# Attention kernel on one NeuronCore: the row maxima enter the shifted scores through the product itself instead of through a second product

## The chip, the cores and the metric

The program runs on 1 core of one Trainium2 chip. The metric is the device time of one execution in microseconds (us), lower is better.

## The reference

Two transformer-like layers over 4096 tokens of width 128, all in fp32. The change lies in the attention of layer 1: 32 sequences of 128 tokens, 16 heads of 8 channels.

```python
x = x + moe0(modulated(x))                      # layer 0: experts, top 2 of 8
x = x + adapter(x)                              # layer 1
h = layernorm(x, ln1_g, ln1_b)
q, k, v = split(h @ w_qkv + b_qkv, 3)           # per head: [128 tokens, 8]
scores = einsum('bhqd,bkhd->bhqk', q, k) / sqrt(8)
attn = softmax(scores, axis=-1)
x = x + einsum('bhqk,bkhd->bqhd', attn, v).reshape(B, S, D) @ w_o + b_o
x = x + moe1(layernorm(x, ln2_g, ln2_b))        # router, top 2 of 8, experts
```

The kernel computes exp(score minus the maximum of its row), so a maximum per query and head must reach the scores before the exponential.

## The kernel before

The program is a row of stages: setup, the router and experts of layer 0, `pre_attention` (adapter, layer norm, queries and keys, written to DRAM), `attention` with the layer norm, router and scatter behind it (`Post`), `experts1`, `finish`. Within a stage each engine runs its own instruction list in the order in which the code writes it; semaphores (`wait_ge`, `then_inc`) join the lists. There is no scheduler.

Inside `attention` the work goes in **laps**, `for s in range(LAPS)`, one lap for each of 32 sequences and 14 more to drain. The 16 heads of a sequence are four groups `g` of four heads. A query or key side of a group is 96 partitions (a high part, a low part and the high part again, 32 rows each, so that one fp32r product is exact enough). What lap s does:

- TensorE (PE), for g = 0 to 3: `score(s + 2, g)`, a 96-row product of queries with masked keys `km` into `ps1`, for the maxima; `shift(s, g)`, the keys `kp` times the masked queries `qm` into `ps2` (line 1721) and then, into the same bank, `selr` times `mxT` (line 1723), which subtracts the maxima. Behind g = 0 stands `mix(s - 1)`, behind g = 3 `total(s - 1)`, 16 small products each. Behind g = 1 stands `turn_max(s + 1)`, four transposes that bring the maxima of the next sequence into `psM`; behind g = 2 `project(s - 2)`.
- VectorE (DVE): `maximum(s + 2, g)` (line 1577, TENSOR_REDUCE of a bank of `ps1` into `mneg`), `invert`, `divide`, `keep` of sequence s - 2.
- ScalarE (ACT): `exponent(s, g)` (line 1662), `copy_max(s + 1)` (line 1648, `psM` to `mxT`, 128x512) between the exponents of g = 1 and 2, and `mask_k(s + 3, j)` for j = 1, 2, 3 (line 1655, `kp` to `km`), the first ahead of the exponent of g = 1, the others behind the copy and behind the exponent of g = 2.
- GpSimd (POOL): `part_max(s + 1)` (lines 1525 and 1527, the maxima split in a high and a low part), `mask_k(s + 3)` for j = 0 (line 1515), `spread_v(s)`, then what the router needs: `post_root`, two indirect scatters (line 472), `post_join`.
- SyncE (SP): in pairs of sequences, 12 loads of `qm` (line 1505) once `shifted` says that the pair two back is done, and then the 6 loads of `qp` and `kp` of the next pair (line 1010).

`score(s, 0)` waits in `ready(s)` for all of `km` of its sequence: for ACT's j = 3 of the lap before it among others. The router work of four sequences is spread over laps by `group(s, after)`. From lap 7 on the laps repeat in four kinds, which the prediction names by letters:

- **T** (s = 7, 11, ...): ACT normalises behind the exponent of g = 2, and PE ends the lap with `post_turn`.
- **S** (s = 8, 12, ...): ACT scales, and PE ends the lap with `post_natural` (line 1403), which uses the banks `psW` and `psM` and waits for `kept` of this lap and for the maxima to have left `psM`.
- **R** (s = 9, 13, ...): DVE takes the logits, ACT copies two row halves (line 461) ahead of its first `mask_k`, DVE picks experts.
- **P** (s = 10, 14, ...): PE ranks, DVE takes statistics and places; its `index_sum` (line 453) gives the indices for which POOL's scatters wait, and `project` waits for DVE's line 436.

Laps 0 to 6 have little or none of that; they are called plain.

```python
for g in range(HG):            # PE, the order within a lap
    if s + 2 < SEQS:
        score(s + 2, g)
    if s < SEQS:
        shift(s, g)
    if behind and g == 0:
        mix(s - 1, range(4))
    if behind and g == 3:
        total(s - 1, range(4))
```

Of the kernel before, what the change touches and what calls it, by code (L numbers as in the profile page):

```python
# [16 lines left out]
P = 128  # L17
SEQS = 32
# [999 lines left out]
def pre_attention(m, d):  # L1018
# [3 lines left out]
    with ExitStack() as ctx:  # L1022
# [29 lines left out]
        with nc.Block(no_gpsimd_drain=True) as block:  # L1052
# [66 lines left out]
            def _(dve):  # L1119
# [23 lines left out]

                dve.wait_ge(m.late_ld, LATE_LOADS)
# [297 lines left out]
def attention_loads(m, ctx):  # L1442

    m.qp, m.kp = ([m.sb(f"{x}{b}", [96, HG, PAIR], F32R, ctx) for b in range(PAIR_BUFFERS)]
                  for x in ("qp", "kp"))
    m.pair_in = m.sems(*(f"a_pair{b}" for b in range(PAIR_BUFFERS)))


def attention(m, d):
# [3 lines left out]
    with ExitStack() as ctx:  # L1453
        sb = lambda n, s, dt=F32: m.sb(n, s, dt, ctx)
        two = lambda n, s, dt=F32: [m.sb(f"{n}{b}", s, dt, ctx) for b in range(2)]
        selr = sb("selr", [P, HG, P], F32R)
        qp, kp, pair_in = m.qp, m.kp, m.pair_in
        qm = two("qm", [96, HG, 4, PAIR], F32R)
# [4 lines left out]
        mxT = two("mxT", [P, 4 * P], F32R)  # L1463
# [6 lines left out]
        (cleared, made, km_pool, km_act, vb_done, scored, maxed, link, parted, turned, mxT_done, shifted,  # L1470
         exped, mixed, divided, projected, kept) = m.sems(
            "a_cleared", "a_made", "a_km_pool", "a_km_act", "a_vb", "a_scored", "a_maxed", "a_link", "a_parted",
            "a_turned", "a_mxT", "a_shifted", "a_exped", "a_mixed", "a_divided", "a_projected", "a_kept")
        qm_in = m.sems("a_qm_in0", "a_qm_in1")
        zeroed = m.sems("a_zeroed0", "a_zeroed1")
# [4 lines left out]
        side = lambda s: (s // 2) % PAIR_BUFFERS  # L1480
        PAIRS = SEQS // 2
# [7 lines left out]
        with nc.Block(no_gpsimd_drain=True) as block:  # L1489
            @block.sync  # L1490
            def _(sp):
                for k in range(PAIRS):
# [16 lines left out]
            def _(pool):  # L1509
                def mask_k(s):  # L1510
# [3 lines left out]
                    for j in range(KM_POOL):  # L1514
                        ins = nc.gpsimd.tensor_scalar(km[s % 2][:, :, j, :], kp[side(s)][:, :, tok(s)].bitcast(F32),  # L1515
# [24 lines left out]
                nc.gpsimd.memset(qm[1][:].bitcast(F32), 0.0).then_inc(zeroed[1], 1)  # L1540
# [29 lines left out]
            def _(dve):  # L1570
# [8 lines left out]

                def invert(s):  # L1580
# [12 lines left out]
                nc.vector.memset(qm[0][:].bitcast(F32), 0.0).then_inc(zeroed[0], 1)  # L1593
                for g in range(HG):
                    ins = nc.vector.tensor_copy(selr[:, g, :], bc(m.const[:, C_SEL + g:C_SEL + g + 1], P, P))
                ins.then_inc(cleared, 1)
                for s in range(2):
                    for g in range(HG):
                        maximum(s, g)
                for s in range(LAPS):  # L1600
# [397 lines left out]
```

## Time and profile before

| what | value |
|---|---|
| median of 3 runs | 771.48 us (765.51 to 772.9) |
| profiled execution, its own time | 765.54 us |
| its span, first to last instruction | 763.7 us |
| attention stage, first score product to the last exponent | about 331 to 557 us of the span |
| busy over the span | PE 79%, DVE 63%, POOL 59%, ACT 50% |
| mean granted TensorE clock | 0.912 of full speed |

Times on the rows of the next section are microseconds from the start of the span, means are ns. PE rows are modelled at their ends, so the distance from the start of one matmul to the start of the next says what it holds of the engine, and its duration says more than that. On a row "[0.20 <-ACT km L1655]" means that the engine had sat idle for 0.20 us and what ended the wait.

### The profile page before, as it was taken

How to read it: one execution, taken by the hardware profiler on the slowest of the kernel's cores; microseconds unless marked ns; L12 is line 12 of the kernel's file. 1: busy time of each engine (PE TensorE's matmuls, PEld its weight loads, DVE VectorE, ACT ScalarE, POOL GpSimd, SP SyncE). 2: the span in 40 equal slices, each digit the busy share in tenths (PEclk: the TensorE clock that was granted, in tenths of full speed). 3: DMA queues.
4: the chain of work that ended last, by engine and by line, in shares of the span. 5: the costliest groups of instructions: out<-in, count | busy, mean ns of one | idle time of the engine just before them, and what ended most of it. 6: DMA issues, size and time to landing. Idle time of an engine off the chain costs nothing. (4 is left out here: it accounts for less than half of the span.)

```text
span 763.7 us, 18100 instructions
## 1 busy us (share of the span) xinstructions
PE 600.0 (79%) x5634; PEld 483.7 (63%) x5634; DVE 480.4 (63%) x1470; ACT 384.6 (50%) x828; POOL 449.0 (59%) x588
## 2 busy tenths in 40 slices
PE   2999935999991767559899989999960699999950
PEld 1566625988991544327666666666740699999950
DVE  2555544766672699655557657656734487878835
ACT  1543403655560334246777777778640365555620
POOL 2477761766677556193545777777666056666650
PEclk9999976999995799959999999999975699999985
DMA  5921155777763168635454563564414988888519
GB/s 162 273 60 49 49 105 153 209 195 205 210 188 113 50 204 220 236 60 88 80 110 71 102 130 81 109 120 93 89 40 99 298 271 242 255 245 253 156 49 317
DMA packets 97833, 115.24 MB, mean 151 GB/s; under 512 B 16128, under 2 KB 77600, under 8 KB 97632
## 3 DMA queue, kind: packets, MB, share of 16 engines
q1 hardware_dynamic: 82224, 92.36, 46.9%
q0 software_dynamic: 9088, 18.76, 7.7%
q10 hardware_dynamic: 6448, 3.20, 1.8%
q8 instruction: 38, 0.62, 0.4%
q14 instruction: 35, 0.29, 0.1%
HBM read 80.75 MB, written 33.53 MB: 150 GB/s over the span
## 5 line engine op out<-in xcount | busy, mean ns | idle before, releaser
L472 POOL DMA_INDIRECT dispatch_rows<-row,index x128 | 128.1, 1000 | 62.4 <-issue 33.9
L1577 DVE TENSOR_REDUCE mneg<-ps 128x4 f32<-128x512 f32 x128 | 87.6, 687 | 77.1 <-PE ps L1711 76.9
L833 POOL DMA_INDIRECT expert_rows<-fo,to x78 | 84.0, 1077 | 68.4 <-DVE fo L1884 55.0
L833 POOL DMA_INDIRECT expert_rows<-eo,to x78 | 74.8, 959 | 50.0 <-ACT eo L926 28.1
L1662 ACT ACTIVATE prob<-ps 128x512 f32<-128x512 f32 x128 | 75.7, 592 | 40.8 <-PE ps L1723 40.3
L806 DVE CAST xh<-psT 128x256 fp32r<-128x256 f32 x78 | 33.1, 425 | 75.6 <-PE psT L774 75.0
L1655 ACT ACTIVATE km<-kp,const 96x512 fp32r<-96x512 f32 x96 | 68.1, 717 | 21.6 <-DMA kp<-qk_parts 10.6
L1711 PE MATMUL ps<-km,qp 96*128 96x512 f32 x128 | 63.7, 504 | 16.7 <-POOL km L1515 11.6
L1873 PE MATMUL psO<-wb,fh 128*128 128x128 f32 x624 | 75.9, 275 | 0.0
L1515 POOL TENSOR_SCALAR km<-kp,const 96x512 fp32r<-96x512 f32 x32 | 54.5, 1702 | 34.9 <-DMA kp<-qk_parts 21.7
L824 PE MATMUL psA<-xh,wh 128*128 128x256 f32 (+1 forms) x234 | 73.5, 314 | 0.0
L1873 PEld LDWEIGHTS psO<-wb,fh 128*128 128x128 f32 x624 | 73.0, 192 | 0.0
L824 PE MATMUL psA<-xh,wl 128*128 128x256 f32 (+1 forms) x234 | 67.1, 287 | 0.0
L824 PE MATMUL psA<-xl,wh 128*128 128x256 f32 (+1 forms) x234 | 66.9, 286 | 0.0
L1721 PE MATMUL ps<-qm,kp 96*128 96x512 f32 x128 | 52.0, 406 | 1.5 <-ACT prob L1662 1.5
L1723 PE MATMUL ps<-mxT,selr 128*128 128x512 f32 x128 | 51.2, 400 | 0.0
L1919 ACT ACTIVATE fw<-psO,xt 128x128 f32<-128x128 f32 x78 | 24.5, 365 | 43.7 <-PE psO L1873 26.2
L798 ACT ACTIVATE wh<-w 128x352 fp32r<-128x352 f32 x39 | 19.4, 497 | 50.3 <-DMA w<-in_W 48.2
L1711 PEld LDWEIGHTS ps<-km,qp 96*128 96x128 f32 x128 | 25.4, 199 | 30.0 <-issue 27.0
L824 PEld LDWEIGHTS psA<-xl,wh 128*128 128x128 f32 (+1 forms) x234 | 43.1, 184 | 0.0
L824 PEld LDWEIGHTS psA<-xh,wh 128*128 128x128 f32 (+1 forms) x234 | 43.0, 184 | 0.0
L824 PEld LDWEIGHTS psA<-xh,wl 128*128 128x128 f32 (+1 forms) x234 | 42.8, 183 | 0.0
(201 smaller groups left out, 1520.7 us busy)
## 6 DMA issues: line engine op xcount, KB each, us to landing
wb<-in_W1b SPq DMA_DIRECT2D x39, 578.0 KB
w<-in_W SPq DMA_DIRECT2D x39, 304.0 KB
qk_parts<-qk SPq DMA_DIRECT2D x8, 1024.0 KB, 5.0
qp<-qk_parts SPq DMA_DIRECT2D x48, 128.0 KB
kp<-qk_parts SPq DMA_DIRECT2D x48, 128.0 KB
qm<-qk_parts SPq DMA_DIRECT2D x192, 32.0 KB
xs<-dispatch_rows SPq DMA_DIRECT2D x39, 130.0 KB
xt<-dispatch_rows SPq DMA_DIRECT2D x39, 130.0 KB
```

The lines of the kernel that those rows point to most:

```text
L472: pool.indirect_dma_start(out=m.xbuf, out_offset=bass.IndirectOffsetOnAxis(ap=r.index[b][:, c:c + 1], axis=0), in_=r.row[b][:, c // TOPK, ...
L806: v.tensor_copy(z.xh[q][:], z.psT[:, q, 0:SLOTS]).then_inc(z.x_high, 1)
L824: ins = z.m.nc.tensor.matmul(out, w[k][q][:, columns], x[k][q][:], start=(k == 0), stop=(k == 2), skip_group_check=True)
L833: pool.indirect_dma_start(out=m.ybuf, out_offset=bass.IndirectOffsetOnAxis(ap=to[b][:, a:a + 1], axis=0), in_=out[b][:, a, :], in_offset=N ...
L1515: ins = nc.gpsimd.tensor_scalar(km[s % 2][:, :, j, :], kp[side(s)][:, :, tok(s)].bitcast(F32), mask(j), None, ALU.mult)
L1577: nc.vector.tensor_reduce(mneg[s % 2][:, g, :], ps1[:, g % 2, :].rearrange("p (j k) -> p j k", j=4), AX_X, ALU.max, negate=True).then_inc( ...
L1655: nc.scalar.activation(km[s % 2][:, :, j, :], kp[side(s)][:, :, tok(s)].bitcast(F32), ACT.Copy, scale=mask(j)).then_inc(km_act, 1)
L1662: nc.scalar.activation(prob[s % 2][:, g, :], ps2[:, g % 2, :], ACT.Exp, scale=ATT_SCALE).then_inc(exped, 1)
L1711: nc.tensor.matmul(ps1[:, g % 2, :], qp[side(s)][:, g, tok(s)], km[s % 2][:, g].rearrange("p j k -> p (j k)"), start=True, stop=True).then ...
L1721: nc.tensor.matmul(ps2[:, g % 2, :].rearrange("p (j k) -> p j k", j=4), kp[side(s)][:, g, tok(s)], qm[(s // 2) % 2][:, g, :, tok(s)], star ...
L1723: nc.tensor.matmul(ps2[:, g % 2, :], selr[:, g, :], mxT[s % 2][:], start=False, stop=True).then_inc(shifted, 1)
L1873: ins = nc.tensor.matmul(psO[:, q, a * P:(a + 1) * P], h[q][:, k, a * P:(a + 1) * P], wb[b][:, WIDE + k * P:WIDE + (k + 1) * P], start=(k ...
```

## The change

`kp` gets 32 more partitions, 96 to 127, which hold ones (three memsets on DVE at the head of its list in `pre_attention`). `qm` gets 32 more partitions too, and into these go the maxima, straight from `psM`. The product of line 1721 then runs over 128 rows and its last 32 add the maxima; `selr`, `mxT` and the product of line 1723 are gone. Since `psM` holds the maxima of group g in partitions 32g to 32g + 31, and all of them must come to 96 to 127, four copies of 32x512 take the place of one of 128x512: those of g = 0 and 1 are `low_maxima` on ACT, at the place of the old copy; those of g = 2 and 3 are `high_maxima` on DVE, behind `maximum` of g = 2 (and the work after it) and behind `maximum` of g = 3. PE waits for each by `low_in` and `high_in`, and `maxima_left` waits for all four before `psM` is written again. One semaphore `zeroed` replaces two, so that the first `qm` loads wait for both memsets of `qm`.

```diff
+                for b in range(PAIR_BUFFERS):
+                    nc.vector.memset(m.kp[b][96:P].bitcast(F32), 1.0)
...
-    m.qp, m.kp = ([m.sb(f"{x}{b}", [96, HG, PAIR], F32R, ctx) for b in range(PAIR_BUFFERS)]
-                  for x in ("qp", "kp"))
+    m.qp, m.kp = ([m.sb(f"{x}{b}", [rows, HG, PAIR], F32R, ctx) for b in range(PAIR_BUFFERS)]
+                  for x, rows in (("qp", 96), ("kp", P)))
...
-        qm = two("qm", [96, HG, 4, PAIR], F32R)
+        qm = two("qm", [P, HG, 4, PAIR], F32R)
-        mxT = two("mxT", [P, 4 * P], F32R)
-        zeroed = m.sems("a_zeroed0", "a_zeroed1")
+        zeroed = m.sem("a_zeroed")
+        maxima_at = lambda s, g: qm[(s // 2) % 2][96:P, g, :, tok(s)]
+        maxima_of = lambda g: psM[32 * g:32 * g + 32, :].rearrange("p (j k) -> p j k", j=4)
...
-                        sp.wait_ge(zeroed[k], 1)
+                        sp.wait_ge(zeroed, 2)
...
+                def high_maxima(s, g):
+                    dve.wait_ge(turned, s + 1)
+                    nc.vector.tensor_copy(maxima_at(s, g), maxima_of(g)).then_inc(high_in, 1)
...
+                    if s + 1 < SEQS:
+                        high_maxima(s + 1, 2)
                     if s + 2 < SEQS:
                         maximum(s + 2, 3)
+                    if s + 1 < SEQS:
+                        high_maxima(s + 1, 3)
...
-                def copy_max(s):
+                def low_maxima(s):
                     act.wait_ge(turned, s + 1)
-                    wait(act, shifted, HG * (s - 1))
-                    nc.scalar.activation(mxT[s % 2][:], psM[:], ACT.Copy).then_inc(mxT_done, 1)
+                    for g in range(2):
+                        nc.scalar.activation(maxima_at(s, g), maxima_of(g), ACT.Copy).then_inc(low_in, 1)
...
                     if g == 0:
                         if s % 2 == 0:
                             pe.wait_ge(qm_in[(s // 2) % 2], 16 * 12 * (s // 4 + 1))
-                        pe.wait_ge(mxT_done, s + 1)
+                    pe.wait_ge((low_in, high_in)[g // 2], 2 * s + g % 2 + 1)
                     wait(pe, exped, HG * s + g - 1)
                     nc.tensor.matmul(ps2[:, g % 2, :].rearrange("p (j k) -> p j k", j=4), kp[side(s)][:, g, tok(s)],
-                                     qm[(s // 2) % 2][:, g, :, tok(s)], start=True, stop=False)
-                    nc.tensor.matmul(ps2[:, g % 2, :], selr[:, g, :], mxT[s % 2][:], start=False, stop=True
-                                     ).then_inc(shifted, 1)
+                                     qm[(s // 2) % 2][:, g, :, tok(s)], start=True, stop=True).then_inc(shifted, 1)
+
+                def maxima_left(count):
+                    wait(pe, low_in, 2 * count)
+                    wait(pe, high_in, 2 * count)
```

On ACT, in lap 9 (kind R), before (row: the rows that go to the scatter, km: masked keys, prob: exponent, mxT: copy of the maxima):

```order
L461 ACTIVATE row10<-psW 128x2x128
L461 ACTIVATE row10<-psM 128x2x128
L1655 ACTIVATE km0<-kp0,const 96x4x128
L1662 ACTIVATE prob1<-ps2 128x512
L1648 ACTIVATE mxT0<-psM 128x512
L1655 ACTIVATE km0<-kp0,const 96x4x128
L1662 ACTIVATE prob1<-ps2 128x512
L1655 ACTIVATE km0<-kp0,const 96x4x128
```

And after:

```order
L461 ACTIVATE row10<-psW 128x2x128
L461 ACTIVATE row10<-psM 128x2x128
L1664 ACTIVATE km0<-kp0,const 96x4x128
L1671 ACTIVATE prob1<-ps2 128x512
L1657 ACTIVATE qm1<-psM 32x4x128 x2
L1664 ACTIVATE km0<-kp0,const 96x4x128
L1671 ACTIVATE prob1<-ps2 128x512
L1664 ACTIVATE km0<-kp0,const 96x4x128
```

Two instructions stand where one stood; everything else keeps its place.

On DVE, in the second half of lap 10 (kind P), before (mneg: maximum, prod, row, index: placing, X3: `keep`):

```order
L1577 TENSOR_REDUCE mneg0<-ps1 128x4
L1347 TENSOR_SCALAR var2<-mv2 128x4
L436 TENSOR_TENSOR base<-base,psW 128x8
L438 TENSOR_TENSOR prod10<-hot10,slot10 128x64
L441 COPY row10<-ids 128x8
L445 TENSOR_SCALAR row10<-tanh10 128x4 x2
L1577 TENSOR_REDUCE mneg0<-ps1 128x4
L453 TENSOR_REDUCE index10<-prod10 128x8
L1591 TENSOR_TENSOR X3<-psW,X3 128x128
```

And after:

```order
L1579 TENSOR_REDUCE mneg0<-ps1 128x4
L1349 TENSOR_SCALAR var2<-mv2 128x4
L436 TENSOR_TENSOR base<-base,psW 128x8
L438 TENSOR_TENSOR prod10<-hot10,slot10 128x64
L441 COPY row10<-ids 128x8
L445 TENSOR_SCALAR row10<-tanh10 128x4 x2
L1584 CAST qm1<-psM 32x4x128
L1579 TENSOR_REDUCE mneg0<-ps1 128x4
L1584 CAST qm1<-psM 32x4x128
L453 TENSOR_REDUCE index10<-prod10 128x8
L1597 TENSOR_TENSOR X3<-psW,X3 128x128
```

Both copies stand ahead of the index, and so ahead of everything that waits for it.

## Rows read from the trace of the kernel before

**Rows 1.** The page, the costliest groups: busy us, mean ns, idle before and releaser.
```profile
L1723 PE MATMUL ps<-mxT,selr 128*128 128x512 f32 x128 | 51.2, 400 | 0.0
```
**Rows 2.** Busy time by stretch: PE, PEld, DVE, ACT, POOL, clock, DMA share, GB/s.
```profile
280.00:300.00 20.00, 14.02 (x81) 9.18 (x80) 17.95 (x47) 7.88 (x15) 10.95 (x14) 1.00 0.65 197
450.00:500.00 50.00, 46.96 (x647) 34.02 (x649) 34.41 (x119) 37.59 (x73) 36.35 (x67) 1.00 0.53 111
```
**Rows 3.** Timeline of the second half of plain lap 2: start, duration, engine, line.
```profile
355.11 0.40 PE L1723 MATMUL ps<-mxT,selr 128*128 128x512 f32 x1
...
355.34 0.60 PE L1730 MATMUL psM<-const,xmx 128*128 128x128 f32 x4
...
356.03 0.59 ACT L1648 ACTIVATE mxT<-psM 128x512 fp32r<-128x512 f32 x1
...
356.51 0.72 ACT L1655 ACTIVATE km<-kp,const 96x512 fp32r<-96x512 f32 x1
...
357.60 0.72 ACT L1655 ACTIVATE km<-kp,const 96x512 fp32r<-96x512 f32 x1
...
358.48 0.50 PE L1711 MATMUL ps<-km,qp 96*128 96x512 f32 x1
```
**Rows 4.** Timeline of lap 21, kind R, and the start of lap 22.
```profile
487.51 0.38 ACT L461 ACTIVATE row<-psW 128x256 f32<-128x256 f32 x1 [0.64 <-DVE logits L325]
...
490.71 0.73 ACT L1655 ACTIVATE km<-kp,const 96x512 fp32r<-96x512 f32 x1
...
491.70 0.47 PE L1711 MATMUL ps<-km,qp 96*128 96x512 f32 x1 [0.20 <-ACT km L1655]
```
**Rows 5.** Timeline from lap 22, kind P, over lap 23, kind T, to lap 24.
```profile
496.49 0.49 PE L1761 MATMUL psW<-wo,oT 128*128 128x128 f32 x2 [0.48 <-DVE base L436]
...
497.25 0.69 DVE L1577 TENSOR_REDUCE mneg<-ps 128x4 f32<-128x512 f32 x1 [0.42 <-PE ps L1711]
...
497.86 0.21 DVE L453 TENSOR_REDUCE index<-prod 128x8 uint32<-128x64 f32 x1
...
498.36 1.09 POOL L472 DMA_INDIRECT dispatch_rows<-row,index  x1 [0.77 <-DVE index L453]
...
498.62 0.50 PE L1711 MATMUL ps<-km,qp 96*128 96x512 f32 x1
...
501.34 0.63 PE L1730 MATMUL psM<-const,xmx 128*128 128x128 f32 x4
...
502.18 0.58 ACT L1648 ACTIVATE mxT<-psM 128x512 fp32r<-128x512 f32 x1
...
506.26 0.47 PE L1711 MATMUL ps<-km,qp 96*128 96x512 f32 x1
```
**Rows 6.** Timeline of the end of lap 20, kind S.
```profile
483.53 0.28 DVE L1591 TENSOR_TENSOR X<-psW,X 128x128 f32<-128x128 f32 x1
...
484.28 0.38 PE L1403 MATMUL psW<-IG,h2T 128*128 128x136 f32 x1
```
**Rows 7.** Timeline of the start of the attention stage, laps 0 and 1.
```profile
332.89 3.50 POOL L1540 MEMSET qm<- 96x4096 f32 x1
...
340.50 1.25 SPq L1010 DMA_DIRECT2D qp<-qk_parts  x3
...
341.40 0.63 PE L1723 MATMUL ps<-mxT,selr 128*128 128x512 f32 x1
...
341.82 0.63 PE L1711 MATMUL ps<-km,qp 96*128 96x512 f32 x1
...
347.19 1.57 POOL L1515 TENSOR_SCALAR km<-kp,const 96x512 fp32r<-96x512 f32 x1 [0.21 <-DMA kp<-qk_parts]
...
349.62 0.60 ACT L1662 ACTIVATE prob<-ps 128x512 f32<-128x512 f32 x1 [0.69 <-PE ps L1723]
```
**Rows 8.** Who waited for whom, 345 to 556 us: total, times, longest.
```profile
ACT km L1655 <- DMA kp<-qk_parts: 10.6, 8, 2.4
```
**Rows 9.** Timeline, DVE's first instruction of the stage `pre_attention`.
```profile
243.01 1.77 DVE L1125 TENSOR_TENSOR part<-gr,X 128x512 f32<-128x512 f32 x1 [13.30 <-DMA gr<-expert_rows]
```

More of the change, by code:

```diff
@@ L1469, in attention @@
         psO = m.ps("psAO", [P, 2, 512], ctx)
-        (cleared, made, km_pool, km_act, vb_done, scored, maxed, link, parted, turned, mxT_done, shifted,
+        (cleared, made, km_pool, km_act, vb_done, scored, maxed, link, parted, turned, low_in, high_in, shifted,
          exped, mixed, divided, projected, kept) = m.sems(
             "a_cleared", "a_made", "a_km_pool", "a_km_act", "a_vb", "a_scored", "a_maxed", "a_link", "a_parted",
-            "a_turned", "a_mxT", "a_shifted", "a_exped", "a_mixed", "a_divided", "a_projected", "a_kept")
+            "a_turned", "a_low_in", "a_high_in", "a_shifted", "a_exped", "a_mixed", "a_divided", "a_projected", "a_kept")
         qm_in = m.sems("a_qm_in0", "a_qm_in1")
-        zeroed = m.sems("a_zeroed0", "a_zeroed1")
+        zeroed = m.sem("a_zeroed")
         post = Post(m, ctx, psW, psM)
@@ L1514, in mask_k @@
                     for j in range(KM_POOL):
-                        ins = nc.gpsimd.tensor_scalar(km[s % 2][:, :, j, :], kp[side(s)][:, :, tok(s)].bitcast(F32),
+                        ins = nc.gpsimd.tensor_scalar(km[s % 2][:, :, j, :], kp[side(s)][0:96, :, tok(s)].bitcast(F32),
                                                       mask(j), None, ALU.mult)
@@ L1539, in _ @@
                 mask_k(1)
-                nc.gpsimd.memset(qm[1][:].bitcast(F32), 0.0).then_inc(zeroed[1], 1)
+                nc.gpsimd.memset(qm[1][0:96].bitcast(F32), 0.0).then_inc(zeroed, 1)
                 for b in range(2):
@@ L1591, in keep @@
                     nc.vector.tensor_tensor(m.X3[:, s, :], psW[:, 0:P], m.X3[:, s, :], ALU.add).then_inc(kept, 1)
[L1593 to L1596, printed above, removed]
+                nc.vector.memset(qm[0][0:96].bitcast(F32), 0.0).then_inc(zeroed, 1)
                 for s in range(2):
@@ L1599, in _ @@
                         maximum(s, g)
+                for g in range(2, HG):
+                    high_maxima(0, g)
                 for s in range(LAPS):
@@ L1654, in mask_k @@
                         wait(act, scored, HG * (s - 1))
-                    nc.scalar.activation(km[s % 2][:, :, j, :], kp[side(s)][:, :, tok(s)].bitcast(F32), ACT.Copy,
+                    nc.scalar.activation(km[s % 2][:, :, j, :], kp[side(s)][0:96, :, tok(s)].bitcast(F32), ACT.Copy,
                                          scale=mask(j)).then_inc(km_act, 1)
@@ L1666, in _ @@
                         mask_k(s, j)
-                copy_max(0)
+                low_maxima(0)
                 for s in range(LAPS):
@@ L1680, in _ @@
                     if s + 1 < SEQS:
-                        copy_max(s + 1)
+                        low_maxima(s + 1)
                     if s + 3 < SEQS:
@@ L1765, in _ @@
                         score(s, g)
-                pe.wait_ge(cleared, 3)
+                pe.wait_ge(cleared, 2)
                 turn_max(0)
@@ L1799, in _ @@
                     if turning is not None:
-                        wait(pe, mxT_done, min(s + 2, SEQS))
+                        maxima_left(min(s + 2, SEQS))
                         wait(pe, post.nat_copied, turning)
@@ L1805, in _ @@
                         wait(pe, kept, min(s - 1, SEQS))
-                        wait(pe, mxT_done, min(s + 2, SEQS))
+                        maxima_left(min(s + 2, SEQS))
                         wait(pe, post.router.slotted, scaling)
```

3 lines of the change are left out of this document (1 added, 2 removed).

## The prediction

> **What bounds the kernel now.** I read the busy table by stretch first, then the timeline of single laps, then the table of waits. Between 450 and 500 us PE is busy 94% of the time, ACT 75%, POOL 73%, DVE 69%, at full clock [rows 2]. That looks like a PE bound, and the product that goes holds 51.2 us of busy time [rows 1]. Both readings are too good. In a plain lap the product of line 1723 starts at 355.11 and the next PE instruction at 355.34 [rows 3]: it holds PE for 0.23 us and not for 0.40. So 128 of them hold PE for 29 us, and this is the most that their removal can give.
>
> Next I ask what lets a lap begin. Its first product, `score(s + 2, 0)`, needs the masked keys of ACT's last `mask_k` in the lap before. In plain lap 2 that one starts at 357.60, takes 0.72 and ends at 358.32; the lap begins at 358.48 [rows 3]. In lap 21 (kind R) it ends at 490.71 + 0.73 = 491.44, and PE stands idle for 0.20 us until it starts at 491.70, released by ACT [rows 4]. ACT reaches that `mask_k` by a chain with no gap in it: transposes on PE (355.34), copy of the maxima (356.03), `mask_k` (356.51), exponent, `mask_k` (357.60). So two chains of about the same length close each lap, PE's own work and this one through ACT. ACT's idle time lies ahead of the chain, where it waits for PE, and can't be used behind it.
>
> **The product that goes.** Each lap PE has four starts of 0.23 us less, 0.92 in all; 0.46 of it lies ahead of the transposes (g = 0 and 1).
>
> **The copies on ACT.** One copy of 128x512 holds ACT for 356.51 - 356.03 = 0.48 us [rows 3]. A copy of 32x512 has as many elements per partition; no row shows one. Below it could cost a quarter, 0.12, if time went by partitions, above 0.59 if it did not overlap with the next. I take 0.48, from the same operation with the same length per partition. The chain of ACT then is 0.48 longer in every lap.
>
> **A plain lap.** The transposes come 0.46 earlier and so does the exponent ahead of the copies; the second copy takes 0.48. The last `mask_k` ends 0.02 later, and the lap's length stays: PE's 0.92 turns into waiting for ACT. Laps 2 to 6: zero.
>
> **A lap R.** Here ACT waits for DVE's logits (487.51, idle 0.64 before it) and copies rows, and from there to the last `mask_k` it has no gap [rows 4]. The logits hang on the first score and on DVE, which the removed product doesn't move. So nothing comes earlier and the second copy counts in full: +0.48. Five such laps (s = 9 to 25; in lap 29 no keys are masked any more): +2.4.
>
> **A lap P.** `project` waits 0.48 for DVE's line 436 (496.49) [rows 5], so three of the four products are hidden by this wait, and the last counts: -0.23. Five laps: -1.2.
>
> **A lap T.** This is where the copies on DVE come in. In lap P DVE has 0.42 us of idle time ahead of its last maximum, and the index starts one maximum later, 497.86 - 497.25 = 0.61 [rows 5]. The two high copies stand ahead of the index. No row shows such a copy; the nearest is a reduce of 128x512 from the same kind of memory, 0.61 from start to start and 0.69 in duration. With 0.61 each the index comes 2 x 0.61 - 0.42 = 0.8 later. Queued behind it: POOL waits for the index (0.77 idle), issues two scatters and only then splits the maxima, after which PE transposes them at 501.34, 3.48 after the index and 501.34 - 498.62 = 2.72 into lap T [rows 5]. PE reaches its transposes at just that time, so there is no slack. After the change they come 2.72 + 0.8 + 0.23 (lap P is shorter) = 3.75 into the lap. The copy follows the transposes by 0.69 as in rows 3, at 4.44 instead of 502.18 - 498.62 = 3.56, which is +0.88, and the second copy adds 0.48: +1.36 on a lap that took 506.26 - 498.62 = 7.64. Four laps (s = 15 to 27): +5.4. In lap 11 ACT waits longest for keys, and I count nothing. ACT's waits for keys are 10.6 us in 8 places, all in laps of odd s [rows 8]; in the other T laps the keys come early enough for a transpose at 3.75.
>
> **A lap S.** `keep` ends at 483.81 and `post_natural` starts at 484.28 [rows 6], when PE is done with `total`. After the change PE would be there 0.92 earlier but waits for `keep`, which stands behind both high copies, and so loses what it won: by the steps of DVE's list (maximum, copy, maximum, copy, keep at 0.61 each from 3.1 into the lap) `keep` ends at 5.8 and `post_natural` starts at 5.9 instead of 5.83. Six laps of +0.07: +0.4.
>
> **The start.** The loads of `qm` for the first pair left as soon as DVE had cleared its buffer; now they wait for POOL's memset, which ends at 336.39. The second pair's twelve loads, which began there before, now come second, and behind them the loads of pair 2, which began at 340.50: a full set of twelve takes 340.50 - 336.39 = 4.1 us of SP's time, so everything behind is 4.1 late. The keys of pair 2, for which POOL waited until 347.19, come at 351.3. ACT masks them ahead of the exponent that started at 349.62 and now starts at 351.9: +2.3, and +0.48 for the copy [rows 7]. Laps 3, 5 and 7 wait for keys anyway [rows 8], whose loads are released by the last shift of the lap two before; they take part of it up, since that shift comes after one product less each time. I count +1.6 of the 2.8.
>
> **The rest.** The three memsets of `kp` are hidden: DVE waits 13.3 us for its first rows there [rows 9]; uncovered they would cost 3 us. Laps 29 to 31 mask no keys, so the product gives something: half of 3 x 0.92, -1.5. The `selr` copies lay in DVE's idle time: nothing.
>
> **The sum**, with 0.61 for a high copy: 1.6 + 2.4 - 1.2 + 5.4 + 0.4 - 1.5 = +7.1. If a high copy does not overlap with its neighbours, each of the four boundaries on DVE loses 0.69 - 0.61 = 0.08, 0.32 per lap, and DVE sets the ends of S, P and T: about 0.96 more per four laps, 5.5 times, +5.3, in all +12.4. Between these ends no row decides; I take the middle, +9.7. On the profiled execution (765.54) this gives 775.2. The three runs have a median of 771.48 and scatter by 1%, and a comparison will be made with runs like these: 771.48 + 9.7 = **781.2**. A measurement of this kernel can tell some 1%, 7.7 us, from no change.
>
> The Trainium skill has a rule that speaks against the copies on DVE: "VectorE: DVE Perf Modes", section "Two Vector instructions with no wait between them", says that an instruction whose input or output starts in another group of 32 partitions than the last one's is held until all earlier ones are done. The copies read from partitions 64 and 96 and write to 96 while their neighbours start at 0. By that rule the upper end, +12.4, holds and the time is 783.9. No row before shows an instruction of this kind between others in this stage, so the trace neither agrees nor disagrees.
>
> **Rivals.** *The copies stand in each other's way (the upper end).* As worked out: 783.9. For it: no two of these instructions share their partitions. Against: nothing in rows. It is the upper half of my forecast; 0.25 of its 0.60.
>
> *PE was the bound and the product's time comes back.* If ACT's second copy is cheap (0.12) or its chain has more slack than I see, plain laps and laps S, R and P give up to 0.92 and T loses little: 26 laps of some 0.6 minus the start's 1.6 is -14, 757. For it: 94% busy [rows 2]. Against: the 0.20 us for ACT in rows 4, while PE does nothing. It decides from an ACT copy under about 0.4 us. Chance 0.10.
>
> *The index chain is absorbed.* If POOL's scatters turn out to wait for something else, laps T cost only the second copy less what the missing product gives, near zero, and the sum is +7.1 - 5.4 = +1.7: 773.2. For it: POOL has 27% idle time. Against: its row names the index as releaser. Chance 0.20.
>
> *The clock falls.* PE's busy share sinks from 94% to about 75%, and each lap T has a gap of over a microsecond more. At the lower level a 512-column product holds PE 341.82 - 341.40 = 0.42 instead of 0.23 [rows 7], and PE's share of a lap would grow by some 3 us; over three or four laps 10 us more, 791. Against: 20 us with PE busy 70% ran at full clock [rows 2]. Chance 0.10.
>
> **How the numbers follow.** Forecast 0.60, of which 0.45 above +7.7 and 0.15 below; clock 0.10; absorbed 0.20; PE bound 0.10, of which 0.09 by over 1%. So faster 0.09, same 0.36, slower 0.55. The range leaves out most of the PE-bound case and the worst of the clock: 769 (+1.7 from a run of before at the low side) to 791.
>
> **What the profile would show.** Right: no line 1723; ACT's two copies of 0.59 each, starting 0.48 apart; laps R 0.48 longer with PE waiting for ACT's km at their ends; laps T near 9 us with PE waiting for POOL's xmx; post_natural waiting for DVE; SP's first qm load at 336.4. Wrong: laps R shorter than 6.48, or copies of 32 partitions under 0.4 us, or DVE's index no later. What would make it wrong in size is the overlap of the high copies and how much of the late start laps 3 to 7 take up.

## The result and the profile after

The changed kernel takes 789.31 us (median of 4 runs, 786.84 to 791.97) against 769.39 for the kernel before in the same comparison (4 runs): ratio 1.027, 95% interval 1.022 to 1.032. Slower was forecast and 789 lies in the range, but the cost is about 20 us where the sum gave 9.7. The profiled execution has a span of 785.0 us against 763.7, so the traces differ by 21.3. Ratios, here and below, leave out runs more than 1.5% above the fastest of the same kernel.

I read three things in this order: where the laps grew, which wait ends each, and what the clock did. A lap is taken from its first score (`score(s + 2, 0)`) to the next one's. "Before" and "after" are the two kernels' traces.

| | before | after | forecast |
|---|---|---|---|
| span's start to first score | 331.5 | 324.5 (-7.0) | 0 |
| first score to start of lap 8 | 61.8 | 66.7 (+4.9) | +1.6 |
| laps R and P together, 5 pairs | 13.40 mean | 14.46 mean (+5.3 in all) | +1.2 |
| laps T, s = 11 to 27 | 7.97 mean | 9.85 mean (+9.4) | +5.4 |
| laps S, s = 8 to 28 | 6.77 | 7.28, three of 8.4 to 8.86 (+7.3) | +0.4 |
| from lap 29 on | 223.0 | 224.35 (+1.3) | -1.5 |

Unrounded, the rows add up to 21.3; the forecast's to 7.1, and 9.7 with half of the price for held copies. Busiest groups of the page of after; they answer to [rows 1] (no second product is left), and columns are the same:

```profile
L1579 DVE TENSOR_REDUCE mneg<-ps 128x4 f32<-128x512 f32 x128 | 87.2, 684 | 52.8 <-PE ps L1720 51.4
...
L1720 PE MATMUL ps<-km,qp 96*128 96x512 f32 x128 | 67.1, 531 | 28.2 <-ACT km L1664 22.4
...
L1730 PE MATMUL ps<-qm,kp 128*128 128x512 f32 x128 | 55.3, 434 | 3.0 <-DMA qm<-qk_parts 2.7
...
L1584 DVE CAST qm<-psM 32x512 fp32r<-32x512 f32 x64 | 44.4, 694 | 2.0 <-PE psM L1741 0.2
L1657 ACT ACTIVATE qm<-psM 32x512 fp32r<-32x512 f32 x64 | 37.5, 585 | 13.1 <-PE psM L1741 11.7
```

A copy of 32 partitions lasts as long as one of 128 on ACT: 585 ns here, 0.59 us for the old 128x512 [rows 3]. On DVE it takes 694 ns, beside 684 for a reduce of 128x512. PE now stands idle ahead of the score for 28.2 us, most of it for ACT's masked keys. Busy time by stretch, after, beside the second row of [rows 2] (the eighth number is the granted clock):

```profile
400.00:450.00 50.00, 36.91 (x544) 25.41 (x542) 40.95 (x125) 38.55 (x70) 26.55 (x52) 0.97 0.45 85
450.00:500.00 50.00, 37.61 (x506) 26.51 (x506) 36.30 (x91) 37.08 (x69) 36.06 (x67) 0.93 0.43 91
500.00:550.00 50.00, 37.79 (x518) 26.53 (x518) 40.45 (x124) 39.10 (x71) 30.07 (x57) 0.94 0.45 88
```

PE is busy 75% of the time instead of 94%, and the clock is no longer 1.00.

**A plain lap.** Timeline of ACT and DVE in lap 2 of after, beside [rows 3]:

```profile
352.85 0.60 ACT L1671 ACTIVATE prob<-ps 128x512 f32<-128x512 f32 x1 [0.41 <-PE ps L1730]
353.47 1.20 ACT L1657 ACTIVATE qm<-psM 32x512 fp32r<-32x512 f32 x2
353.52 0.69 DVE L1579 TENSOR_REDUCE mneg<-ps 128x4 f32<-128x512 f32 x1
354.24 0.69 DVE L1584 CAST qm<-psM 32x512 fp32r<-32x512 f32 x1
354.69 0.72 ACT L1664 ACTIVATE km<-kp,const 96x512 fp32r<-96x512 f32 x1
354.96 0.69 DVE L1579 TENSOR_REDUCE mneg<-ps 128x4 f32<-128x512 f32 x1
355.43 0.60 ACT L1671 ACTIVATE prob<-ps 128x512 f32<-128x512 f32 x1
355.68 0.70 DVE L1584 CAST qm<-psM 32x512 fp32r<-32x512 f32 x1
355.93 0.71 ACT L1664 ACTIVATE km<-kp,const 96x512 fp32r<-96x512 f32 x1
356.74 0.47 PE L1720 MATMUL ps<-km,qp 96*128 96x512 f32 x1 [1.20 <-issue]
```

Read starts, not durations. Exponent to first copy takes 353.47 - 352.85 = 0.62, the two copies to the mask 1.22, the mask to the exponent 354.69 to 355.43 = 0.74. With the kernel before, copy to mask was 0.48 and a mask's step 0.61. So around the copies, which write at partition 96 where the others write at 0, ACT loses its overlap, 0.12 to 0.13 at each of four steps, and the chain is 1.0 us longer instead of 0.48. The fourth step, mask to exponent, is longer although both write at partition 0; the exponent reads its bank at partition 0, and the last that ACT had read from such a bank was the second copy, at 32. No run takes the reading apart from the writing. DVE's steps are 0.72 where they were 0.61.

**R, P and T.** The timeline of after from lap 21 (kind R) to lap 24, beside [rows 4, 5]:

```profile
503.89 0.70 DVE L1584 CAST qm<-psM 32x512 fp32r<-32x512 f32 x1
504.62 0.51 DVE L411 TENSOR_TENSOR diff<-best 128x4 f32<-128x4 f32 x1
504.73 0.47 PE L1720 MATMUL ps<-km,qp 96*128 96x512 f32 x1 [1.65 <-ACT km L1664]
...
509.60 0.15 DVE L436 TENSOR_TENSOR base<-base,psW 128x8 f32<-128x8 f32 x1
509.81 0.49 PE L1772 MATMUL psW<-wo,oT 128*128 128x128 f32 x2 [1.43 <-DVE base L436]
...
511.70 0.51 PE L1720 MATMUL ps<-km,qp 96*128 96x512 f32 x1
512.33 0.22 DVE L453 TENSOR_REDUCE index<-prod 128x8 uint32<-128x64 f32 x1
512.84 1.09 POOL L472 DMA_INDIRECT dispatch_rows<-row,index  x1 [2.01 <-DVE index L453]
515.79 0.66 PE L1741 MATMUL psM<-const,xmx 128*128 128x128 f32 x4 [1.67 <-POOL xmx L1529]
```

PE waits 1.65 for ACT's keys at the end of R; 1.43 for `base` in P instead of 0.48; and 1.67 for the spread maxima in T. The index comes 7.60 us into lap P instead of 6.16, POOL waits 2.01 for it, and the turn comes 4.09 into lap T instead of 2.72: the chain the prediction laid out, with larger links. PE's last wait in T is for ACT's norming, which stands behind the copies and the exponent of g = 2: 2.10 in laps 11 and 19, where laps T of before had 0.81 to 1.46. So a T lap is the late turn, then ACT's chain with its dearer copies, then the norming.

**The start.** Timelines of POOL, PE and DVE at the first scores, after:

```profile
322.56 3.12 POOL L1517 TENSOR_SCALAR km<-kp,const 96x512 fp32r<-96x512 f32 x2 [12.99 <-POOLq L1052]
...
324.53 1.19 PE L1720 MATMUL ps<-km,qp 96*128 96x512 f32 x2 [7.46 <-ACT km L1664]
```

and before:

```profile
325.41 7.52 POOL L1515 TENSOR_SCALAR km<-kp,const 96x512 fp32r<-96x512 f32 x2 [12.99 <-POOLq L1052]
326.21 3.47 DVE L1593 MEMSET qm<- 96x4096 f32 x1 [5.08 <-PEq L1052]
329.60 0.97 DVE L1595 CAST selr<-const 128x128 fp32r<-128x128 f32 x4
```

Of the 7.0 us, 2.85 are an earlier start of POOL's work here (325.41 against 322.56), which is scatter of the stages before: in the other traces of changed kernels from the chips where the kernel before takes 767 us, that start lies between 323.7 and 327.2. The other 4.1 I had not foreseen: the first two masks take 3.12 us instead of 7.52.

### The profile page after: what moved, and what is told of

Its sections match the earlier page's. It is cut to its first block and busy times, and to the rows that moved or that the text cites. A ratio compares the mean times of both kernels' runs of the same rounds, so it can differ in the third digit from the quotient of the medians.

```text
span 785.0 us, 18011 instructions
## 1 busy us (share of the span) xinstructions
PE 587.7 (75%) x5506; PEld 469.6 (60%) x5506; DVE 527.9 (67%) x1533; ACT 411.8 (52%) x860; POOL 446.5 (57%) x588
## 5 line engine op out<-in xcount | busy, mean ns | idle before, releaser
L1720 PE MATMUL ps<-km,qp 96*128 96x512 f32 x128 | 67.1, 531 | 28.2 <-ACT km L1664 22.4
L1517 POOL TENSOR_SCALAR km<-kp,const 96x512 fp32r<-96x512 f32 x32 | 50.0, 1563 | 28.9 <-DMA kp<-qk_parts 15.6
L1730 PE MATMUL ps<-qm,kp 128*128 128x512 f32 x128 | 55.3, 434 | 3.0 <-DMA qm<-qk_parts 2.7
L1584 DVE CAST qm<-psM 32x512 fp32r<-32x512 f32 x64 | 44.4, 694 | 2.0 <-PE psM L1741 0.2
L1657 ACT ACTIVATE qm<-psM 32x512 fp32r<-32x512 f32 x64 | 37.5, 585 | 13.1 <-PE psM L1741 11.7
```

The lines of the kernel that those rows point to most:

```text
L1584: nc.vector.tensor_copy(maxima_at(s, g), maxima_of(g)).then_inc(high_in, 1)
L1657: nc.scalar.activation(maxima_at(s, g), maxima_of(g), ACT.Copy).then_inc(low_in, 1)
L1720: nc.tensor.matmul(ps1[:, g % 2, :], qp[side(s)][:, g, tok(s)], km[s % 2][:, g].rearrange("p j k -> p (j k)"), start=True, stop=True).then ...
L1730: nc.tensor.matmul(ps2[:, g % 2, :].rearrange("p (j k) -> p j k", j=4), kp[side(s)][:, g, tok(s)], qm[(s // 2) % 2][:, g, :, tok(s)], star ...
```

## The experiments

Twelve kernels. e1 to e4 ran on one chip and i1 on another, where the kernel before takes 842 to 844 us (there the first score stands at 382 to 394 us instead of 324 to 329, and behind lap 29 it takes 236 to 246 us instead of 222 to 224); the other seven ran on two where it takes 767 to 768. So laps are compared over all, ratios within one chip.

**e1: DVE's copies at partition 0.** DVE's two copies write to rows 0 to 31 of a spare tile and read psM from partition 0; rows 96 to 127 get other maxima than they should and the exponent is scaled down so that it stays finite.

```diff
-  nc.vector.tensor_copy(maxima_at(s, g), maxima_of(g))
+  nc.vector.tensor_copy(idle[:, g % 2], psM[0:32, :].rearrange(...))
```

> The two copies on DVE keep their number, place and size, but read partitions 0 to 31 of the maxima bank and write to partitions 0 to 31 of a spare tile; ACT's two copies read partitions 64 and 96. The maxima of two groups are left out and the exponent's scale is 0.01 of the right one, so the output is not the reference's. Theory A (an instruction whose input or output starts in other partitions than its neighbours' doesn't overlap with them): on DVE, start to start falls from 0.72 to 0.61 for each copy and its neighbours, 0.4 us per lap; laps S shrink from 7.28 by about 0.3, laps T by up to 0.4, laps R stay at 7.48 because ACT sets them; in all 4 to 6 us less than the changed kernel. Theory B (a copy of this size just costs its 0.69): DVE's steps and the time stay within 1 us of the changed kernel, 20 us above the kernel before.

Measured: 867.13 us, ratio 1.025 (1.020 to 1.030). DVE in lap 20, timeline:

```profile
560.34 0.67 DVE L1585 CAST idle<-psM 32x512 fp32r<-32x512 f32 x1
560.94 0.67 DVE L1580 TENSOR_REDUCE mneg<-ps 128x4 f32<-128x512 f32 x1
561.54 0.67 DVE L1585 CAST idle<-psM 32x512 fp32r<-32x512 f32 x1
562.14 0.27 DVE L1598 TENSOR_TENSOR X<-psW,X 128x128 f32<-128x128 f32 x1
```

The same number of copies with the same elements, and a step is 0.60 instead of 0.72: what costs is the change of partition. Laps without a clock fall: S 6.76 to 6.79 (from 7.28), P 6.69 at the least (6.98), T 9.26 (9.74), plain laps unchanged, R 7.50 in two of five. The other three R take 8.08 to 8.16 at full clock, with PE waiting 1.0 to 1.1 for DVE's `oT`. Such laps, with that wait, stand in e2, e3, e4 and i1 too, only on the two chips with the slower stages, and no run explains them. The held copies cost S all of its +0.51. That theory A holds is read from the laps; no changed kernel ran on this chip to hold the total against.

**e2: ACT's copies at partition 0.** The same edit for the two copies on ACT, with the same parts of the result left out.

> The two copies on ACT read partitions 0 to 31 and write to partitions 0 to 31 of a spare tile, number, place and size as in the changed kernel. The maxima of two groups are left out and the exponent's scale is 0.01 of the right one. Theory A: ACT's steps from the exponent over both copies and the masked keys to the next exponent fall from 0.62 + 0.61 + 0.61 + 0.74 = 2.58 to 0.49 + 0.48 + 0.48 + 0.61 = 2.06, so laps R go from 7.48 to 6.96, plain laps from 6.30 to about 5.9, laps T by 0.5; in all about 12 us less than the changed kernel. Theory B (the copy itself is slow at 32 partitions): ACT's steps stay, and so does the time.

Measured: 870.52 us, ratio 1.028 (1.023 to 1.033). ACT in a plain lap, timeline:

```profile
415.47 1.05 ACT L1658 ACTIVATE idle<-psM 32x512 fp32r<-32x512 f32 x2
416.42 0.71 ACT L1665 ACTIVATE km<-kp,const 96x512 fp32r<-96x512 f32 x1
417.04 0.57 ACT L1672 ACTIVATE prob<-ps 128x512 f32<-128x512 f32 x1
```

Two copies in 0.95, mask to exponent 0.62: the overlap is back. Plain laps take 5.75 and R 6.92. So ACT has the same price, and in plain laps it is the whole of the +0.48. But the ratio is where it was (1.027). Where R is 6.92, P is 7.54 at its shortest, and 6.92 + 7.54 = 14.46, the same as 7.48 + 6.98; most later P laps took about 9.1, with the clock at half. I read only the second at the time; the first came back in f3.

**e3: an empty product in the removed one's place** (zeros, 128 by 512, one behind each shifted product), so that PE works as before.

> Behind each shifted score product stands again a second one of 512 columns, of zeros, so PE holds what it held before; all else is the changed kernel. It adds nothing to the values. Theory C (part of the loss is the clock, which in the changed kernel fell to half for 3.4 us at a time, six times within the attention stage, since PE idles more): the clock stays at 1.00 over the stage, the S laps of 8.4 to 8.85 us become 7.3, and the time falls by 4 to 6 us against the changed kernel though there is more work. Theory D (PE is close to the path, the clock doesn't matter): the time rises by some 3 to 10 us.

Measured: 880.02 us, ratio 1.040 (1.036 to 1.045). Plain laps 6.78, S 7.77 at the least, P 7.22, T 9.5, R 7.47 at the least. PE's busy share is 83% in 450 to 550 us. The clock still fell, three times between laps 8 and 29 (seven times in e4's trace, from the same chip). So it fell less often, as theory C had it, but not never, and the time rises, by 9.5 us over e4's: theory D holds. The product is worth some 0.5 us in plain laps and S and nothing in R; the 0.24 that P grows by, T gives back (9.50 instead of 9.74). Keeping PE busier with it costs more than it could save.

**e4: one wait for each of the two cleared buffers** instead of one for both, as the kernel before has it.

```diff
-  sp.wait_ge(zeroed, 2)
+  sp.wait_ge((zeroed, cleared)[k], 1)
```

> The first loads of qm wait for their own memset alone again, those of the second pair for the other, as before the change; all else is the changed kernel. My account of the changed kernel's start: PE waited 2.67 us for the first qm loads and ACT 1.42 us for the keys of pair 2, so the time falls by 2 to 3 us. If laps 3, 5 and 7 take up what the start loses, it falls by under 1 us.

Measured: 870.52 us, ratio 1.030 (1.025 to 1.036). Lap 0 falls from 9.24 to 7.19 and PE's wait for `qm` from 2.67 to 0.38, yet from the first score to lap 8 it takes 66.41 us against 66.67 in the trace of after. That comparison misleads: in e4 the clock fell in lap 4 (7.59 instead of 6.31) and was at half for longer in lap 1. e1, on the same chip with the same waits as after and the clock at half in the same laps, takes 68.65. Against it e4 saves 2.2, nearly all in lap 0, and the laps behind do not take it up; the expected 2 to 3 us are there, though the ratio, by another chip's after, can't show them.

**a0: the changed kernel again**, unedited, beside f1 to f3.

> The changed kernel itself, unedited, as the yardstick for the three edits that run beside it on this chip. Theory A (each copy pays for its start partition, and the longer lap comes from four places: R +1.0, S +0.5, T about +1.9, clock drops about 1.5 each): ratio to the kernel before 1.022 to 1.032, laps R 7.48, S 7.28 or about 8.8 with a clock drop, T 9.7, P 6.98. Rival D (the ratio of one chip does not carry to another, because the other stages move too): ratio outside 1.02 to 1.035 with laps of the same lengths.

Measured: 791.26 us, ratio 1.028 (1.021 to 1.035); laps as forecast (R 7.48, T 9.74, S 7.28 or 8.8).

**f1: in laps P, both high copies behind the index sum.**

```diff
-  if s + 1 < SEQS:
+  if s + 1 < SEQS and placing is None:
       high_maxima(s + 1, 2)
...
   if placing is not None:
       index_sum(r, dve, placing)
+  if s + 1 < SEQS and placing is not None:
+      for g in range(2, HG):
+          high_maxima(s + 1, g)
```

> Only the laps that place tokens (kind P) are changed: both high copies stand behind the index sum instead of ahead of it. Theory A (the turn of lap T is late because the index sum, the scatters behind it and with them the spread of the next maxima on GpSimd are late): index sum back at about 6.2 us into lap P, turn at about 3.0 into lap T instead of 4.14, lap T about 8.3 to 8.5 instead of 9.7, five times, so 6 to 7 us less than the changed kernel beside it, some 1 us of it given back where lap P's own third and fourth products now wait for the late copies. Rival E (the turn of lap T is late for its own work, the norming on DVE ahead of the copies, and the index chain has slack): lap T stays within 0.3 of 9.7, the total within 1 us of the changed kernel or above it.

Measured: 781.7 us, ratio 1.018 (1.011 to 1.026), 9.6 under a0. Timeline of laps 22 and 23, which begin at 501.14 and 508.12:

```profile
507.60 0.21 DVE L453 TENSOR_REDUCE index<-prod 128x8 uint32<-128x64 f32 x1
507.84 1.42 DVE L1584 CAST qm<-psM 32x512 fp32r<-32x512 f32 x2
508.10 1.09 POOL L472 DMA_INDIRECT dispatch_rows<-row,index  x1 [0.84 <-DVE index L453]
510.76 0.23 POOL L1529 TENSOR_TENSOR xmx<-mneg,xmx 128x16 f32<-128x16 f32 x1
511.05 0.66 PE L1744 MATMUL psM<-const,xmx 128*128 128x128 f32 x4 [0.50 <-POOL xmx L1529]
```

Index at 6.46 into P, POOL's wait 0.84, turn at 2.93 into T, T 8.57 to 8.59 every time instead of 9.74. Theory A holds and rival E falls: moving two copies past one instruction of 0.2 us gives back 1.15 in a lap T. Between laps 8 and 29 f1's trace is 11.4 us shorter than a0's: 4.6 of it in laps T (one of a0's, behind a slow P, took 8.50), and 6.8 in laps S and P, where the clock fell. f1's fell once there, a0's six times, one of them twice as long.

**f2: ACT's low copies behind the last mask**, in all laps but T. **f3: both orders.**

```diff
-  if s + 1 < SEQS:
+  if s + 1 < SEQS and norming is not None:
       low_maxima(s + 1)
...
   if s + 3 < SEQS:
       mask_k(s + 3, 3)
+  if s + 1 < SEQS and norming is None:
+      low_maxima(s + 1)
   if s < SEQS:
       exponent(s, 3)
```

> ScalarE's two low copies stand behind the last key mask of the lap and ahead of the fourth exponent, in all laps but T. Theory A (in plain laps and in R the next lap's first score waits for the last key mask, which the two copies of 0.61 hold back): R from 7.48 to 6.3 to 6.5, plain from 6.3 to 5.3 to 5.7, S from 7.28 to 6.8 to 7.0, in all 5 us for R, 3 for the plain laps, 1 to 3 for S: 8 to 11 us less than the changed kernel, less where the clock falls oftener. Rival F (what the masks gain the first shifted product of the next lap loses, since it waits for the low copies that are now last): R and plain laps stay within 0.2 and PE waits for the low copies instead of the masks, total within 1.5 us.

> Both reorderings at once. Theory A says that they work in different laps and add up: 13 to 17 us under the changed kernel, ratio to the kernel before 1.004 to 1.013. Theory C (below a certain share of busy time on PE the clock falls more often, so that time taken out of the laps by reordering comes back as clock drops): no more than the larger of the two alone, with more stretches at half clock than in the changed kernel. Against both, a version faster than the kernel before would need more than 20 us.

Measured: f2 793.18 us, ratio 1.032 (1.026 to 1.037); f3 782.54 us, 1.018 (1.012 to 1.024). R is 5.99 in both, shorter still than theory A had it, and nothing comes of it. f3's laps P are 8.47 where the clock stays up, and 5.99 + 8.47 = 14.46 once more. Timeline of PE in that lap:

```profile
443.92 0.49 PE L1777 MATMUL psW<-wo,oT 128*128 128x128 f32 x2 [1.91 <-DVE base L436]
```

`base` comes 12.37 us after the start of the lap R before (431.34 to 443.71) in f3 and 12.36 (431.86 to 444.22) in f1. What R wins, P waits, and f3 gives no more than f1 alone. Theory C forecast that, but not for this reason; neither A nor F said it; the bound is DVE's list, see below. Behind that, from lap 18 of f3 and in all rounds of f2, the clock falls in P, T and S: P 10.03, S 8.80, T 9.33. Timeline of PE in such a lap P of f2, with the score at 0.80 us instead of 0.48:

```profile
485.00 0.79 PE L1774 MATMUL psW<-wo,oT 128*128 128x128 f32 x2 [1.90 <-DVE base L436]
485.44 0.77 PE L1722 MATMUL ps<-km,qp 96*128 96x512 f32 x1
...
488.44 0.80 PE L1722 MATMUL ps<-km,qp 96*128 96x512 f32 x1
```

**h1: f1 and the late low copies in R and plain laps only. h2: h1 and, in T, the residual add ahead of the last high copy.**

> f1 (both high copies behind the index sum in P) with the low copies behind the last key mask in laps of kind R and in the plain laps 0 to 6 alone. In f3 the same order in S and P as well brought one or two falls of the clock into P and one into S and T of nearly every four laps. Theory C1 (it was the order in S and P that did it: there the low copies came late for the next lap's first shifted product, and the hole beside the waits of T let the clock fall): R 5.99, plain 5.5 to 6.0, S 7.28, T 8.59, P 6.98, at most three falls between laps 8 and 29, 7 to 9 us under f1, so about 773 and a ratio of 1.006 to 1.012. Rival C2 (the clock falls for the shorter R, whatever the place of the copies elsewhere): S, P and T of 8.5 to 10 as in f3, total within 2 us of f1's ratio 1.018.

> h1, and in laps of kind T the residual add (keep) stands ahead of the last high copy on DVE instead of behind it. Theory A (a copy of 0.72 on DVE holds back whatever stands behind it by its full length; PE waits 1.24 to 1.5 us for this add at the end of lap T in f1): that wait falls to 0.5 to 0.8 and T from 8.59 to 7.9 to 8.1, five times, 2.5 to 3.5 us less than h1. Rival G (the add waits for its product and not for the copy): T within 0.15 of h1, no change in the total.

Measured: h1 797.41 us (four times: 784.0, 797.0, 797.9, 798.6; no ratio, since only one would count); h2 785.34 us, ratio 1.021 (1.014 to 1.029). In the traces of both (797.9 and 794.2 us) R is 5.99, P 10.03, T 9.3 and S 8.8 in nearly every round. C1 had about 773 and at most three falls; h1's best is 784.0. So C1 falls: with the copies of S and P back in their place the clock still fell. What the 784.0 looked like inside, no trace shows. h2's edit rested on a wrong reading: the wait of 1.24 us for the add that I had put at the end of T stands at the end of S, so the edit was in the wrong lap.

**i1: h2's edit alone on f1.**

```diff
+  if inner and norming is not None:
+      keep(s - 2)
   if s + 1 < SEQS and placing is None:
       high_maxima(s + 1, 3)
```

> f1 with the one edit of h2 (the residual add ahead of the last high copy in laps T), and the order on ScalarE as in the changed kernel, so that R stays at 7.48. Theory C2 (it was the R lap of 5.99, which puts PE's holes of P, T and S closer together, that let the clock fall in nearly every four laps of f3, h1 and h2): R 7.48, T 8.0 to 8.1, S 7.28, P 6.98, so 29.8 for four laps, at most three falls of the clock between laps 8 and 29, and 2 to 3 us under f1's ratio of 1.018: 1.013 to 1.017. Rival J (the clock falls whenever four laps take less than f1's 30.3): S and P of 8.5 to 10 in at least three of the five rounds of four laps, ratio of 1.02 or more.

Measured: 863.25 us, ratio 1.026 (1.021 to 1.031), on a chip that neither f1 nor a0 ran on. R 7.48 at the least and T 8.59 to 8.68 in four of six laps (8.32 in the other two), so the add gives nothing there (h2's rival G). The timelines say why: in lap 11 the add moves from 6.76 to 5.94 us into the lap, but PE's last wait in T is for ACT's norming, whose last instruction starts at 7.25 in f1 and 7.33 in i1 (i1's trace names DVE's last copy for it, which had ended at 6.95). The clock fell six times between laps 8 and 29 though R was not shortened, so C2 as put falls as well; the ratio alone would speak for rival J, but four laps were not shorter than f1's either. On the clock this run decides nothing.

**g2: the kernel before, with the four copies that build `selr` behind the first eight maxima.**

```diff
-  for g in range(HG):
-      ins = nc.vector.tensor_copy(selr[:, g, :], ...)
   for s in range(2):
       for g in range(HG):
           maximum(s, g)
+  for g in range(HG):
+      ins = nc.vector.tensor_copy(selr[:, g, :], ...)
```

> The kernel before, with one edit: the four copies on DVE that build the selecting matrix stand behind the first eight maxima instead of ahead of them. The changed kernel, which has no such copies, started its first scores about 4 us earlier for the first key masks on GpSimd, 3.12 us instead of 7.52. Theory H (these four copies, beside which GpSimd's first mask runs, are what slows it): the two first masks on GpSimd 3.1 to 3.3 us, first score 3 to 4.5 us earlier against the start of the stage, total 2 to 4 us less, ratio 0.995 to 0.998. Rival I (the first mask on GpSimd is slow for the DMA or for other work of the stage before): still 7.0 to 7.6 us and a ratio of 0.999 to 1.001.

Measured: 764.96 us (10 runs) against 767.65 (13 runs), ratio 0.9953 (0.9912 to 0.9995). Timeline of POOL and DVE:

```profile
326.47 3.12 POOL L1515 TENSOR_SCALAR km<-kp,const 96x512 fp32r<-96x512 f32 x2 [13.02 <-POOLq L1052]
327.27 3.47 DVE L1593 MEMSET qm<- 96x4096 f32 x1 [5.08 <-PEq L1052]
...
330.66 0.62 DVE L1577 TENSOR_REDUCE mneg<-ps 128x4 f32<-128x512 f32 x1
```

Theory H holds: the first score stands 1.97 behind POOL's start instead of 6.07, and 1.6 of these 4.1 us are lost again by lap 8. This is the one version below both kernels, by half a per cent, with the interval's end so near 1 that the gain in the total is hardly shown.

## Why the prediction was right, and where its sizes were wrong

**Right.** PE was not the bound: 128 products gone and from lap 8 on no lap is shorter. The chain from the copies through the index, the scatters and the spread to the turn is there (f1). ACT's last mask ends the plain laps (f2's are down to 6.0). The removed product is worth half a microsecond in a lap at most (e3). That 789 lies in the range is partly luck: by its own terms the forecast ended at 783.9, and the range went on to 791 for the clock, whereas more of the excess came from terms priced too low (10.3 us against the clock's 6.2, see below), and the unforeseen gain at the start hid a part of it.

**The copies on ACT** (forecast +0.48 in the chain): +1.00. I priced a copy like its neighbours, 0.48 from start to start, and wrote nothing of the boundaries around it. e2, where the copies stay at partition 0, shows that they are what the other 0.5 is. So "the lap's length stays" in plain laps fails: 6.30 against 5.82.

**The copies on DVE** (0.61, upper end 0.69): 0.72 a step, as the upper end had it, and a short instruction behind a copy pays as well: `diff` takes 0.44 to its successor (504.62 to 505.06) instead of 0.07. The Trainium skill's rule ("VectorE: DVE Perf Modes", section "Two Vector instructions with no wait between them") was in the forecast as its upper half; e1 agrees with it, 0.60 against 0.72. For ACT the skill's "ScalarE: Activation LUTs", section "What ACT_TABLE_LOAD costs", gives an overlap of some 93 ns between neighbours and no condition for it; here the overlap was about 0.11 (0.59 - 0.48, [rows 3]) and gone around the copies.

**R and P** (forecast +0.48 - 0.23 a pair): +1.07. This is the step that failed in its mechanism, not in its size. I let `base` stay where it was and put P's wait for it down as a cover. But `base` closes a list on DVE that begins in R with the logits, and three instructions of it (`diff`, `hot`, `mask`) stand behind both high copies, the ranking on PE behind them. Timeline of DVE before:

```profile
487.32 0.16 DVE L325 TENSOR_TENSOR logits<-psM,rows 128x16 f32<-128x16 f32 x1
...
492.27 0.69 DVE L1577 TENSOR_REDUCE mneg<-ps 128x4 f32<-128x512 f32 x1 [0.78 <-PE ps L1711]
...
496.28 0.16 DVE L436 TENSOR_TENSOR base<-base,psW 128x8 f32<-128x8 f32 x1
```

That is 8.96 us with 1.28 of idle time (0.17, 0.33 and 0.78). After, logits at 499.34 and `base` at 509.60 are 10.26 apart with 0.56 idle: two copies of 0.72, 0.12 more for the maximum between them and 0.37 more at `diff` are 1.9 of work, and 0.72 less waiting pays for a part of it. From R to P DVE became the bound, and PE's wait at R's end, which I had read as ACT's doing, could be removed without effect (e2 and f3: R + P = 14.46 where the clock stays up). Only cheaper copies on DVE shorten the pair (e1: 14.19).

**T** (+1.36, four laps): +1.88, five laps. The index came 1.44 later and not 0.8. `base` was late already, the 0.42 of idle time I credited was gone, and each copy takes 0.72. Without that chain (f1) T is 8.59, 0.6 above before, with ACT's dearer copies in it. Lap 11, which I excluded for its late keys, grew by 0.87, the other four by 1.72 to 2.71 (2.24 without the clock's part).

**S** (+0.07): +0.51, all of it the held copies (e1).

**The start** (+1.6): +4.9 from the first score to lap 8. The late loads are 2.2 of it (e4 beside e1), near the 2.3 I had before I took off what laps 3 to 7 would absorb; they absorb next to none of it. By an estimate from g2 about 1.6 is what the earlier first score costs by lap 8; the rest is about 1 us, with +0.48 in laps 2 and 4 from the copies on ACT. What I wrote off, "the `selr` copies lay in DVE's idle time: nothing", was wrong: POOL's first two masks gain 4.4 us, and the first score stands 2.0 us behind their start instead of 6.1, in after and in g2.

**The clock**, a rival at 0.10, came in addition to the forecast's mechanisms. Six stretches of 3.4 us at half clock between 390 and 551 us, none there before. Three lie in laps S (1.12, 1.53 and 1.58 over 7.28) and three in laps T, where two cost nothing, since PE's wait for the norming shrinks from 2.10 to 0.62 and 0.54, and one 0.47. Together they cost 4.7 us; the rival had 10.

**From lap 29 on** (-1.5; half of 3 x 0.92 is 1.4): +1.3. A seventh stretch, 571.1 to 574.5, falls into lap 30, and the last exponent stands 18.16 us behind the start of lap 29 instead of 16.47. In a0 and f1, without it, that is 16.65 and 16.69. So the clock took 1.5 more, and the missing product gave nothing there either.

Of the 22.0 us in laps 8 to 28, then: the list on DVE over R and P 5.3; T's chain 8.9, of which f1 gives back 1.15 in each of five laps; held copies in S 3.1; clock 4.7. Over the whole span the traces differ by 14.2 us more than the 7.1 of the sum: R and P 4.1, T 3.5, S 2.7, the clock 6.2, from lap 29 on 1.3 without it, and 3.6 less for the start, where 2.85 are the scatter of the stages before.

**Left open** is what makes the clock fall. It isn't PE's mean busy share: f1 has 75% (112.5 of 150 us) and one fall, e3 83% and three, and f3 held its clock over two rounds that are as long as f1's (30.3) and lost it in all after them. Nor is it one long wait alone: PE's longest between laps 8 and 29 is 2.2 us in f3 and 2.1 in f1. Where the falls come in every round, four laps take 34.1 to 34.2 us in f2, f3, h1 and h2 alike.

## What to carry to other kernels

Count an added instruction on every engine at its step from start to start with its own neighbours on both sides, and where it starts at other partitions than they do, take the overlap away twice. A wait that seems to cover a saving must be followed to what releases it: if that engine is given work too, there is no cover. And where two chains close a stretch at the same time, shortening the one that the wait names gives nothing; look for the sum over laps that doesn't change.

## What the runs showed of the hardware

ScalarE loses the overlap of neighbouring instructions around copies that start at another group of 32 partitions, as VectorE does: steps of 0.62, 0.61, 0.61 and 0.74 us in after where e2 has 0.49, 0.48, 0.48 and 0.61.

Four copies on DVE slow a mask on POOL that began long before them: the first mask took 5.97 us instead of 1.57, from 325.41, while the copies ran from 329.60 to 330.57 behind a memset from 326.21. With the copies elsewhere the same memset slows nothing (g2). By the times it is as if POOL had done half of the mask up to 326.21, stood still until 330.57 and done the other half then; how, no run here shows. The Trainium skill ("SBUF — State Buffer", section "Who interferes with whom") says that a VectorE instruction which takes both of its port pairs and a GpSimd instruction shut each other out, and that the one which issues first has the shared pair until it ends. Whether these copies are of that kind, no run shows; here it was the mask, which had started first, that was stretched, and the copies behind it were done before it.

TensorE's clock can fall to half for single stretches of 3.4 us while PE is busy 75% of the time. A stretch costs 1.1 to 1.6 us in a lap S and 0 to 0.5 in a lap T, where PE would have waited anyway. The four versions whose laps R are shorter by order (f2, f3, h1, h2) have falls in most rounds, which cost more than R had won; that the shorter R sets them off is not shown, and i1 had six falls with R at its old length.
